# Cross-attention scores of two heads in the two row halves of TensorE

## The reference, cut to what matters

```python
logits = einsum('bhqd,bhkd->bhqk', q_h, k_h) * scale            # 77 text keys
text_out = einsum('bhqk,bhkd->bhqd', softmax(logits), v_h)
scores = einsum('bhqd,bhkd->bhqk', q_h, ip_k_h) * scale         # 179 image keys
text_probs = softmax(einsum('bqc,bkc->bqk', q, k_text) * scale)
sem = einsum('bqc,bnc->bqn', text_probs @ text, ip) * scale
ip_probs = softmax(scores + 0.5 * sem[:, None]) * spatial_mask  # sem is added for every head
out = (text_out + ip_probs @ ip_v) @ Wout + bout + residual
```

## Time and profile before

| | us |
|---|---|
| Median of 3 runs (lowest, highest) | 1666.56 (1665.37, 1671.36) |
| Span of the profiled execution | 1665.6 |
| PE busy, weight loads | 1599.7, 1424.2 |
| DVE, ACT, POOL busy | 1376.6, 992.3, 844.8 |

### The profile page before, as it was taken

The page is one execution under the profiler, slowest core; times in us unless marked ns, Lnnn a source line. Parts: engine busy times, 40 slices in busy tenths (PEclk is TensorE's granted clock), DMA queues, the critical chain, the costliest instruction groups (busy, mean ns, idle before and its releaser), DMA issues.

```text
span 1665.6 us, 42402 instructions
## 1 busy us (share of the span) xinstructions
PE 1599.7 (96%) x14248; PEld 1424.2 (86%) x14248; DVE 1376.6 (83%) x3937; ACT 992.3 (60%) x2044; POOL 844.8 (51%) x789
## 2 busy tenths in 40 slices
PE   6999999999999999998989999999999999999986
PEld 5888888888888888788878998989998989998866
DVE  4688788888888888867879998999999998998874
ACT  3455565555556555655656666666666666666651
POOL 3224422222222323424767676777667776777662
PEclk9999999999999999999999999999999999999988
DMA  8334444444444444542323332333233323332201
GB/s 223 97 105 121 129 121 124 124 129 125 120 129 124 124 128 122 144 123 75 112 88 87 100 95 80 102 106 99 66 109 102 100 67 101 101 103 63 79 22 43
DMA packets 204225, 175.31 MB, mean 105 GB/s; under 512 B 45441, under 2 KB 203531, under 8 KB 204011
## 3 DMA queue, kind: packets, MB, share of 16 engines
q1 hardware_dynamic: 204010, 172.60, 35.8%
HBM read 112.13 MB, written 60.38 MB: 104 GB/s over the span
## 4 chain that ended last, share of the span: by engine, by line
PE 88%; DVE 6%; issue 3%; DMA 1%; SPq 1%; ACT 1%; POOL 0%; DVEq 0%; POOLq 0%; ACTq 0%
PE MISC L103 26%; PE GP L103 20%; PE NAT L265 10%; PE TR L278 8%; PE PV L324 5%; PE PV L309 4%; PE PV L306 3%; PE PV L327 2%; PE MISC L227 2%; PE MISC L367 1%; DVE ZP L895 1%; PE MISC L368 1%; PE MISC L466 1%; DVE TMP L779 1%; PE MISC L388 1%
## 5 line engine op out<-in xcount | busy, mean ns | idle before, releaser
L540 ACT ACTIVATE P<-TA 128x512 f32<-128x512 f32 x320 | 202.6, 633 | 279.4 <-DVE TA L888 278.0
L984 POOL TENSOR_TENSOR ZS<-ZP 128x256 f32<-128x256 f32 x267 | 255.4, 957 | 210.4 <-DVE ZP L895 209.0
L265 PE MATMUL NAT<-KS,QS 65*128 65x256 f32 x1280 | 300.1, 317 | 3.6 <-DMA KS<-qk_parts 2.1
L103 PE MATMUL GP<-PH,GH 128*128 128x256 f32 (+1 forms) x960 | 248.8, 288 | 20.9 <-DVE ZP L895 19.9
L278 PE MATMUL TR<-QS,KS 69*128 69x256 f32 (+1 forms) x1280 | 259.9, 285 | 4.6 <-DMA QS<-max_rows 2.5
L783 DVE TENSOR_REDUCE MX<-NAT 128x2 f32<-128x504 f32 x320 | 216.6, 677 | 51.3 <-PE NAT L265 46.9
L901 DVE SCALAR_TENSOR_TENSOR PM<-P,PH 128x512 f32<-128x512 f32 x320 | 255.3, 798 | 0.0
L215 POOL TENSOR_TENSOR PARTS<-QKF,PARTS 112x508 fp32r<-112x508 f32 (+3 forms) x93 | 119.3, 1283 | 265.1 <-ACT PARTS L568 263.2
L265 PEld LDWEIGHTS NAT<-KS,QS 65*128 65x128 f32 x1280 | 201.2, 192 | 56.9 <-issue 42.1
L103 PE MATMUL GP<-PH,GL 128*128 128x256 f32 (+1 forms) x960 | 243.0, 281 | 0.0
L543 ACT ACTIVATE P<-TR 128x512 f32<-128x512 f32 x320 | 192.7, 602 | 74.3 <-PE TR L278 71.3
(11 more groups left out here) (253 smaller groups left out, 3886.9 us busy)
## 6 DMA issues: line engine op xcount, KB each, us to landing
QS<-qk_parts SPq DMA_DIRECT2D x480, 64.0 KB
KS<-qk_parts SPq DMA_DIRECT2D x480, 64.0 KB
qk_parts<-PARTS SPq DMA_DIRECT2D x128, 224.0 KB, 2.8
CT<-in_ctx_t SPq DMA_DIRECT2D x32, 512.0 KB, 3.9
qk_parts<-PARTS SPq DMA_DIRECT2D x64, 192.0 KB, 2.4
XT<-in_x_t SPq DMA_DIRECT2D x48, 112.0 KB, 2.6
XT<-x_t SPq DMA_DIRECT2D x48, 112.0 KB, 2.4
XB<-in_x SPq DMA_DIRECT2D x16, 320.0 KB, 4.1
```

The costliest lines, as they stand in the source:

```text
L103: ins = e.matmul(out, lhs, rhs, start=(n == 0), stop=(n == len(pairs) - 1))
L265: ins = e.matmul(NAT[s % 2][:, i * T:(i + 1) * T], QS[0:KQ, h, i * 128:(i + 1) * 128], KS[0:KQ, h, :], start=True, stop=True)
L540: e.activation(P[:, s % NP, :], TA[:, s % 2, :], ACT.Exp, scale=SCALE).then_inc(q["exp"], 1)
L984: e.tensor_tensor(ZS[s % NZ][:, :], ZP[:, s % 2, 0:S], ZP[:, s % 2, S:2 * S], ALU.add).then_inc(q["zs"], 1)
```

## The change

`QS` and `KS` become tiles of 128 partitions in which an even head lies in rows 0 to 51 and an odd head in rows 64 to 115, with a buffer for each parity of the batch. The zeroing of `QS` and `KS` (L731, L971) goes, since the maximum's rows follow the parts directly. PE no longer issues two products of `NAT` and two of `TR` in each slot, but in every second slot those of two heads, the upper and the lower half alternately. `LEAD` becomes 12. The condition of this block is that both heads before have left both banks of `NAT`, and of `TR`.

In stage 0 DVE adds the semantic term for even heads only; for odd heads ACT copies `TR` to `TA` in SBUF and POOL adds `ST` there. SP's six stack DMAs of a group become twelve with half the heads each, and the reading back of the maxima becomes two DMAs. With the new `LEAD` the write of the maxima stands at slot `4g - 6` and their reading back at `4g - 4`, ahead of the stack of group `g + 3` at the same slot. Some smaller lumps move by one slot.

```diff
-QS, KS = sb("QS", [TRK0, H, S], F32R), sb("KS", [TRK0, H, T], F32R)
+QS, KS = sb("QS", [128, 2, H // 2, S], F32R), sb("KS", [128, 2, H // 2, T], F32R)
-LEAD, ROWS = 11, 2
+LEAD, ROWS = 12, 2
...
+    def of_head(s, rows):
+        b, h = divmod(s, H)
+        r0 = HALF_PE * (h % 2)
+        return QS[r0:r0 + rows, b % 2, h // 2, :], KS[r0:r0 + rows, b % 2, h // 2, :]
...
+            heads = [s for s in (t + LEAD, t + LEAD + 1) if t % 2 == 0 and 0 <= s < 2 * S1]
+                if s:
+                    e.wait_ge(q["mx"], s)
+            scores = [s for s in (t, t + 1) if t % 2 == 0 and 0 <= s < 2 * S1]
+                if 0 < s <= S1:
+                    e.wait_ge(q["sum"], s // 2)
+                    e.wait_ge(q["trc"], s // 2)
+                elif s > S1:
+                    e.wait_ge(q["exp"], s)
+            for i in range(2):
+                for s in heads:
+                    qs, ks = of_head(s, KM)
+                    ins = e.matmul(NAT[s % 2][:, i * T:(i + 1) * T], qs[:, i * 128:(i + 1) * 128], ks, start=True, stop=True)
+            for i in range(2):
+                for s in scores:
+                    qs, ks = of_head(s, TRK0 if s < S1 else TRK1)
+                    ins = e.matmul(TR[s % 2][:, i * S:(i + 1) * S], ks[:, i * 128:(i + 1) * 128], qs, start=True, stop=True)
...
 ACT, stage 0
+                if s == t and t % 2 == 0 and 0 <= t < S1:
+                    e.wait_ge(q["tr"], t + 2)
+                    e.copy(TA[:, 1, :], TR[1][:, :]).then_inc(q["trc"], 1)
 POOL, stage 0
+            if t % 2 == 0 and 0 <= t < S1:
+                e.wait_ge(q["trc"], t // 2 + 1)
+                e.tensor_tensor(TA[:, 1, :], TA[:, 1, :], ST[:, b % 2, :], ALU.add).then_inc(q["sumo"], 1)
 DVE, stage 0
-            if 0 <= s < S1:
+            if 0 <= s < S1 and s % 2 == 0:
 SP
                 for i, dst, parts in ((0, QS, Q_PARTS), (1, KS, K_PARTS)):
-                    e.dma_start(dst[16 * r:16 * r + 16, h0:h1, :].bitcast(F32),
-                                parts_h[b % 2, i, parts[r], D * h0:D * h1, :].rearrange("(h d) t -> d h t", d=D)).then_inc(q[f"stack{hg}"], 16)
+                    src = parts_h[b % 2, i, parts[r], D * h0:D * h1, :].rearrange("(j a d) t -> a d j t", a=2, d=D)
+                    for half in range(2):
+                        r0 = HALF_PE * half + 16 * r
+                        e.dma_start(dst[r0:r0 + 16, b % 2, 2 * hg:2 * hg + 2, :].bitcast(F32), src[half]).then_inc(q[f"stack{hg}"], 16)
```

More of the change, by code:

```diff
@@ L219, in _ @@
         for t in range(T0, T1):
-            for off, lo, hi, width in ((HG + 4, 0, G1, 4), (HG + 5, G1, 2 * G1, 2)):
+            for off, lo, hi, width in ((HG + 5, 0, G1, 4), (HG + 5, G1, 2 * G1, 2)):
                 g = due_group(t, off, lo, hi)
@@ L252, in _ @@
                 ins.then_inc(q["stm"], 1)
-            s = t + LEAD
-            if 0 <= s < 2 * S1:
-                b, h = divmod(s, H)
+            heads = [s for s in (t + LEAD, t + LEAD + 1) if t % 2 == 0 and 0 <= s < 2 * S1]
+            if heads:
+                s = heads[0]
                 if s == 0:
                     e.wait_ge(q["w_rest"], 3 * 16)
[L258 to L271, removed]
-                    e.wait_ge(q[f"mrow{s // HG % 2}"], mrows(s // HG))
[L273 to L280, removed]
+                if s % HG == 0:
+                    e.wait_ge(q[f"stack{s // HG % NGRP}"], stacked(s // H + 1))
@@ L524, in _ @@
                     e.wait_ge(q["mx"], H * (b - 1))
-                    e.wait_ge(q["sum"], H * (b - 1))
+                    e.wait_ge(q["sum"], H // 2 * (b - 1))
+                    e.wait_ge(q["sumo"], H // 2 * (b - 1))
                 e.wait_ge(q["snm"], b + 1)
@@ L529, in _ @@
                 e.copy(ST[:, b % 2, :], ring.bank["st", b][:, :]).then_inc(q["st"], 1)
-            s = t
-            if 0 <= s < 2 * S1:
+            for s in ([t - 1] if t % 2 == 0 and t <= S1 else []) + ([t] if t % 2 == 0 or t >= S1 else []):
+                if s == t and t % 2 == 0 and 0 <= t < S1:
+                    if t:
+                        e.wait_ge(q["exp"], t)
+                    e.wait_ge(q["tr"], t + 2)
+                    e.copy(TA[:, 1, :], TR[1][:, :]).then_inc(q["trc"], 1)
+                if not 0 <= s < 2 * S1:
+                    continue
                 if s == 0:
@@ L887, in _ @@
                 e.wait_ge(q["tr"], s + 1)
-                e.tensor_tensor(TA[:, s % 2, :], TR[s % 2][:, :], ST[:, b % 2, :], ALU.add).then_inc(q["sum"], 1)
+                e.tensor_tensor(TA[:, 0, :], TR[0][:, :], ST[:, b % 2, :], ALU.add).then_inc(q["sum"], 1)
             s = t - 2 - S1
@@ L1135, in _ @@
             if g is not None:
[L1136 to L1141, removed]
+                b, hg = divmod(g, NGRP)
+                n = 2 if g < G1 else 1
+                e.wait_ge(q[f"mxw{g % 2}"], 16 * (g // 2 + 1))
+                rows = rows_h[g % 2].rearrange("(part grp c) q -> part grp c q", part=2, grp=2)
+                for half in range(2):
+                    r0 = HALF_PE * half + KM
+                    src = rows.rearrange("part grp (j a i) q -> part grp a j (i q)", j=2, a=2)[:, 0:n, half, :, :]
+                    e.dma_start(QS[r0:r0 + 2 * n, b % 2, 2 * hg:2 * hg + 2, :].bitcast(F32),
+                                src.rearrange("part grp j q -> (part grp) j q") if n == 2 else src[:, 0, :, :]).then_inc(q[f"mrow{g % 2}"], 16)
             g = due_group(t, -4 * HG)
@@ L1146, in _ @@
                     e.wait_ge(q[f"spilled{m}"], 32 * (b + 1))
[L1147 to L1148 removed]
+                if b >= 2:
+                    e.wait_ge(q["tr"], HG * (g - 2 * NGRP) + HG)
                 stack(b, hg)
[L1150 to L1152 removed]
+                if b in (B, B + 1):
+                    for r0 in (0, HALF_PE):
+                        e.dma_start(KS[r0 + KM:r0 + TRK1, b % 2, 2 * hg:2 * hg + 2, :].bitcast(F32),
+                                    sel_h[4:6, :].unsqueeze(1).broadcast_to([2, 2, T])).then_inc(q[f"stack{hg}"], 16)
             for m in range(3):
```

47 lines of the change are left out of this document (28 added, 19 removed).

## The result

The changed kernel is slower, and by far more than predicted: a median of 1887.72 us (1886.56 to 1891.59, 4 runs) against 1666.12 (1665.37 to 1671.36, 4 runs) for the kernel before. The ratio is 1.133, its 95% interval 1.131 to 1.135. The prediction, 1717 us with a range to 1765, had the direction and not the size: +51 was forecast, +221 came.

What follows compares the result with a forecast made beforehand. PE was taken to bound both stages, with SP's issuing to set stage 0 after the change. 1665.6 + 65 (stage 0) - 19 (stage 1) + 5 (start and stage change) = 1716, 1717 against the median; range 1631 to 1765.

Steps and rivals of the forecast that it cites:

- SP's sum for stage 0: SP's DMA issues and waits in stage 0 take 47.2 us a batch against 43.1 before: +65 us.
- The reading back: SP's issuing of the maxima's reading back in stage 0: ten at 0.37, 3.7 us a batch.
- The landing: SP's wait for the written maxima to land: 1.33 to 1.72 us beyond the 0.62 issue, 1.7 taken.
- The price of a stack DMA that carries half: On SP, a stack DMA step still costs 0.466 us with half the bytes; bounds 0.33 and 0.466.
- rival 1: SP: issuing is not the bound, a step costs less for half the bytes, kernel faster at 1631 us; chance 0.16.
- The waits of the block: PE's paired block waiting until both heads before are reduced: priced at nothing.
- My cover argument: Stage 0, two slots: DVE's 3.3 us fits in PE's over 4.1, so the block's waits cost nothing.
- PE's saving: Pairing in row halves saves PE 0.12 us net in two slots, 1.2 a batch; bounds +0.36 to -0.55.
- rival 3: PE: halves overlap fully and switching is cheap, 0.36 us saved in two slots; 1679 us; chance 0.15.
- rival 2: PE: the halves don't work at the same time, stage 1 pays the switches, +40 us; 1777 us; chance 0.12.
- Stage 1: Stage 1 gains PE's 1.2 us a batch, -19 us in all; SP's work fits there and costs nothing.
- rival 4: The block's waits or SP's in stage 1 bind as well, stage 1 unchanged or slower; 1736 to 1752 us; chance 0.12.

Runs made afterwards that it cites:

- e4: The kernel before with SP's part alone: twelve stack DMAs a group, maxima read back by two DMAs ahead of the stack; 1842.8 us, ratio 1.107.
- e1: The changed kernel with the maxima read back behind the stack of the same slot instead of ahead of it; 1792.7 us, ratio 1.078.
- e2: The changed kernel with groups 1 and 2, and 3 and 4, stacked together: 36 stack DMAs a batch instead of 60; 1831.9 us, ratio 1.101.
- e8: The kernel before with PE's block of two heads every second slot alone, in the old rows, DVE adding for every head; 1766.7 us, ratio 1.060.
- e3: The changed kernel with both 36 stack DMAs a batch and the maxima read back behind the stack; 1740.5 us, ratio 1.045.
- e10: The changed kernel with 36 stack DMAs a batch, maxima read back behind the stack in stage 0, ahead of it in stage 1; 1731.5 us, ratio 1.038.
- e6: e3 with the block's eight products issued head by head, so that list neighbours use the same half of the rows; 1751.1 us, ratio 1.051.
- e9: Changed kernel without blocks: each slot alternates NAT and TR of two heads in opposite halves; DVE adds every head, 36 stack DMAs; 1778.1 us, ratio 1.068.
- e7: e3 with DVE adding the semantic term for every head, ACT's copy and POOL's addition removed; 1848.5 us, ratio 1.108.

## Why the prediction was wrong, point by point

**The step that failed by most is SP's sum for stage 0**: 47.2 us a batch were predicted, 55.6 measured, that is +198 instead of +65. The mechanism was right: sixty issues and a wait between write and reading back, all in one order, PE idle at a group's first `NAT` with a stack DMA named, the wait for `NH` gone. Its terms were all somewhat small. One batch, 388.23 to 442.73 us, is 54.5, split by the starts of SP's issues:

| | predicted | measured |
|---|---|---|
| write to reading back, with `XT` and `x_t` between (3.1 + 5.7 + 2.8) | 11.6 | 3.20 + 2.29 + 2.23 + 3.78 + 2.13 = 13.6 |
| reading back, 10 | 3.7 | 5 x 1.36 = 6.8 |
| stack, 60 | 28.0 | 29.7 |
| spills, `CT` and single ones | 3.9 | 4.4 |
| sum | 47.2 | 54.5 |

The reading back was the worst estimate. I took 0.37 from a DMA of `4x1024` (0.32); the new one is `4x2x256`:

```profile
L1164 SPq DMA_DIRECT2D QS<-max_rows x90: 603/609/637, 203.7 to 693.2; - x90
```

The landing was priced with 1.33 to 1.72 beyond the issue, and took about that behind a spill (2.23 - 0.62 = 1.6) and behind the store of `x` (2.13 - 0.62 = 1.5); behind the load of `CT` write to reading back took 3.78, 1.5 more than the estimate has. The price of a stack DMA that carries half is as predicted:

```profile
L1124 SPq DMA_DIRECT2D QS<-qk_parts x270: 310/423/1818, 205.1 to 698.0; - x135
```

0.42 us as before for half the bytes; rival 1 is out. The stack is above 28.0 by a few stalled issues, such as 403.07, where two took 1.41. e4 confirms the whole term apart from PE: SP's part alone costs 178 us. It doesn't part the sixty issues from the early reading back; on the changed kernel e1 takes the one away (-95 us) and e2 24 of the issues (-56).

**The waits of the block, priced at nothing, are the second failure.** e8 puts the block at 100 us on the old kernel, and e3 and e10, with most of SP's cost removed, still lose 74 and 65. Of e10's 65, the batches of the table are (1.6 + 1.1) x 16 = 43; another 17 lie in the first batch (56.1 us where it was 39.3), which no run takes apart. My cover argument compared sums over two slots (3.3 us of DVE against 4.1 of PE). It had the condition, both heads before reduced, but a sum doesn't show when in the two slots the second reduction ends: in e3 PE stood for it 22 times in 500 us, 1.05 us each. The two banks by which PE ran a head ahead of DVE are used up by the pair. In stage 1 `GP` waits for `ZP`, which I had called covered, and the block costs 2.1 us a batch.

**PE's saving was about as predicted.** The pair overlaps fully, and 0.67 us for two heads against 0.69 for one bears out rival 3's first half; rival 2 is out. From the start of the last other product to the start of the next one the block takes 0.88 us; e8's block of eight in the old rows takes 1.07:

```profile
1202.57 0.28 PE L103 MATMUL MISC<-XTSL,WQH 112*96 112x256 f32 x1
...
1203.64 0.28 PE L103 MATMUL GP<-PH,GH 128*128 128x256 f32 x1
```

So PE saves 0.19 in two slots, and 0.08 to 0.09 where the next full product comes late as well (1201.89 to 1202.12), around the predicted 0.12. By the same distance the four products of one head took about 0.61 in the kernel before, two heads 1.21; the slot without a block keeps a step of 0.12, so the block saves 1.21 - 0.88 - 0.12 = 0.21. What this time was worth in the whole is open, since e6 doesn't take the overlap away. The switch costs what the Trainium skill, "TensorEngine Tiling (Array Packing)", Key Properties, says it must: changing the mode drains the engine. The trace agrees and prices it, in steps that are otherwise 0.12: 0.21 us in, 0.22 from the first pair to the second, 0.21 out, and 0.20 (e9's rows) to 0.23 to the next full product.

**Stage 1** was forecast at -19 and SP's work there at nothing. It came out 0.7 us a batch longer, some 11 us, so rival 4 held there in kind. SP has time there and is not the bound; its longest wait in 1300 to 1600 us is that for `NH`, 23.1 us in 13 times.

PE's saving of 1 to 2 us a batch and the block's cost (2.1 by e8), with a little lost clock (0.99), leave about what was measured.

**Moved work.** POOL's addition took 1277 ns and ACT's copy 587 (predicted 1280 and 571), and neither is on the path; e7 shows that they even help. The prediction gave DVE's relief no worth, since PE was the bound; but e7, e3 without it, is 108 us slower, since the block waits for DVE.

**The parts don't add up**: 178 (e4) and 100 (e8) are more than 221, as they can be where the waits of one engine cover those of another: while PE waits for a late stack, DVE catches up and frees the banks. e8 also keeps a sum on DVE that the change takes away. In the other direction, the change without SP's cost is +65 (e10), so SP's share is 221 - 65 = 156 by that count, 178 by e4 and 221 - 100 = 121 by e8, and in each the larger. I had the chances of "SP's waits" and "the block's waits" as alternatives (rival 4, to 1752); the range should have held both at once. The Trainium skill, "DMA: Bandwidth & Descriptors", Issuing engines are not separate DMA queues, calls the time to initiate a DMA usually small beside the DMA; in e4 that time, 0.47 us sixty times, is 28 of a batch that had 43, and with the round trips of the maxima in the same list it is the bound.

## What to carry to other kernels

Before a change doubles the number of DMAs, sum the issuing engine's list for one period, with the price of each DMA's exact shape, and let it stay well below the period: where a wait for a round trip to memory stands in that list, it adds in full, and everything behind it is late. When two items are packed into one step, ask which buffers must then be free together; double buffering for single items is no buffering for pairs, and a sum of busy times doesn't show it. Time saved on the engine that was the bound can be less than the new waits ahead of it, so price these first. And look in the trace whether an experiment's edit did on the engine what it says: the order of a list is not always the order in which PE starts.

## What the runs showed of the hardware

**The price of an issue went by shape, not by bytes.** On SP, in medians: `4x2x256` took 609 ns, `2x2x256` (stage 1) 254, a stack DMA of 16 rows 423 with 32 KB, where the row of before shows 0.43 with 64 KB. Two of `4x512` in e4, with the bytes of two of `4x2x256`, took 264 ns each in the median.

Why four rows with two pieces each cost more than sixteen stays open.

**Row halves of PE work fully side by side**: products of 48 rows and 52 rows in the two halves start 0.00 us apart (e9's rows), a block of eight takes 0.88 us instead of 1.07, and the price is in going in and out. The order in the list doesn't matter to it: issued head by head (e6), the other half's first product still starts 0.007 us behind, ahead of the second product of its own half, which stands before it in the list.

**A wait of 2 us cost clock as well.** In e3, stage 1, PE stood 2.03 us at a block, waiting for the maxima; the products from 1.2 us behind its start on are 0.21 us apart instead of 0.12:

```profile
1298.54 0.51 PE L279 MATMUL NAT<-KS,QS 48*128 48x256 f32 x4 [2.03 <-DMA QS<-max_rows]
...
1299.94 0.41 PE L104 MATMUL GP<-PH,GH 124*128 124x256 f32 x1
1300.15 0.41 PE L104 MATMUL GP<-PH,GL 124*128 124x256 f32 x1
```

The granted clock in that stretch (0.83), with the one ahead of it:

```profile
1280.00:1296.00 16.00, 16.00 (x157) 13.93 (x159) 14.10 (x32) 9.91 (x20) 10.41 (x11) 1.00 0.54 159
1296.00:1306.00 10.00, 7.60 (x60) 6.78 (x52) 5.42 (x12) 5.30 (x15) 6.33 (x7) 0.83 0.23 64
```

PE fell to the lower of its two levels, 1.2 GHz, for a part of these 10 us. In stage 0 of the changed kernel the granted clock is 0.89 on average, which is (1 - 0.89) x 2 = 22% of the time at 1.2 GHz, against none before. A late stack thus is paid twice: by the wait, and by slower products behind it.
